# A new edge stage in a four-layer graph network: duplicate keys by products of sign codes, a scatter with split sources

## The chip, the cores and the metric

The kernel runs on one core of one Trainium2 chip. The metric is the time of one execution in microseconds (us). The engines are PE (TensorE, with PEld for its weight loads), DVE (VectorE), ACT (ScalarE), POOL (GpSimd) and SP, whose queue issues all transfers here. PE's clock has two levels, 1.2 and 2.4 GHz; the granted clock in a row is a share of the higher one.

## The reference

512 nodes with 512 features, and 16384 edges (src, dst, weight), sorted by dst. Four layers follow one another, each with a residual and a layer norm. The edges enter all of them, and the kernel turns them into two dense 512 x 512 matrices first: W_SD, the bias of the first attention, and A_SD, the number of edges between two nodes. The bias is *set*, not added: of several edges with the same (dst, src) the last one counts.

```python
src, dst = (edge_index[0], edge_index[1])
bias = jnp.full((n, n), NEG, dtype=x.dtype)
bias = bias.at[diag, diag].set(0.0)
bias = bias.at[dst, src].set(edge_weight.astype(x.dtype))
...
scores = jnp.einsum('hnd,hmd->hnm', q, k) / np.sqrt(HEAD_DIM)
attn = jax.nn.softmax(scores + bias[None, :, :], axis=-1)
```

The other layers are a mean over neighbours, a second attention with a mask, and a sum over neighbours; the change leaves them as they are.

## The kernel before

The program is written engine by engine, each with its own order, and semaphores between them. A ring of four PSUM banks carries all products of the dense layers in a fixed order (`ring_order`); `claim` takes the next bank when its last content is evacuated. Four other banks (`bank`) serve the edge stage and later the attention.

The 16384 edges are 128 tiles of 128. Two tiles make a group (64 groups); the edges are sorted by dst, so a group's dst lie in a window of 32 columns whose start is found at run time. Four groups make one round of the loops (16 rounds). The edge stage has these parts:

- **Keys** (L691 to L719). DVE casts src and dst to fp32, makes a key 512 dst + src, finds the range of each tile and from it the window starts, packed for the loops. SP stores the keys in DRAM (L324) and reads them back spread to all partitions, 8 MB in five pieces (L329). PE turns src, dst, weight and key so that an edge lies on a partition (L1023).
- **Duplicates** (L739 to L767). For every tile, DVE compares the key on the partition with the keys of this tile and the next one of its group, masked to later edges, and accumulates (L743, 128 instructions). An edge with a later equal key gets weight 0. Weights are kept as three bf16 parts, since a bf16 product would round them; POOL (L384) and DVE multiply them into one-hots of the window column (`rhs`).
- **Dense work beside it.** PE makes Q (L1031), K, V (L1002) and all 32 score products S (L1049); ACT evacuates them. The scores go to the tile G, in which the spread keys lie, so ACT waits for the compares.
- **Scatter** (L1052 to L1081, in loops). For each group PE multiplies a one-hot of the source (512 columns, in four blocks `b` of 128) with the window one-hots and the three weight parts, 24 bf16 matmuls. DVE makes one of the source one-hots (L781) and copies the window one-hots (L782); ACT makes the other in two steps (L552, L557). Then ACT copies the counts (L578), POOL adds them to A_SD (L438), and DVE clears the touched places of W_SD (L797) and adds the new weights (L804, the fold).

After the last fold `bias_built` lets PE turn W_SD and A_SD (L1008), DVE takes row minima of score plus bias (L847), ACT the exponentials, and the layers follow. SP loads x after `bias_built` too, POOL adds the bias to V (L429) in the middle of its weight products and makes the residual sums (L458) once x is there.

The order of PE's work around the change is the order of these lines: the range product, the turns of the edges, Q, the spread of the window starts, K, V, S, scatter. On SP's queue it is: edges, x and W_q by blocks, keys out, keys back with W_k and W_v between the pieces, W_o, W_1, vectors.

Of the kernel before, what the change touches and what calls it, by code (L numbers as in the profile page):

```python
# [7 lines left out]
I32 = mybir.dt.int32  # L8
# [17 lines left out]
KEY_CHUNKS = [0, 1, NI // 4, NI // 2, 3 * NI // 4, NI]  # L26
# [12 lines left out]

def ring_order():  # L40
# [9 lines left out]
    for b in range(NB):  # L50
        add("V", (b,), "A")
    for h in range(H):
        for b in range(NB):
            add("S", (h, b), "A")
# [66 lines left out]
def gnn_program(nc, a, out):  # L121

    ctx = ExitStack()
    with ctx:
# [6 lines left out]
        key_dram = nc.dram_tensor("key_scratch", [NT, P], FP32, kind="Internal").ap()  # L131
# [8 lines left out]
        WAF = sb("WAF", [P, 4 * NB * D + 2 * GI * 2 * WIN])  # L140

        WA = WAF[:, 0:4 * NB * D].rearrange("p (w b n) -> p w b n", w=4, b=NB)
        XT = WA[:, 3, :, :]

        rhs = WAF[:, :].bitcast(BF16).rearrange("p (t k n) -> p t k n", t=NT + 2 * GI, k=4)
# [47 lines left out]
        minus_src = sb("minus_src", [P, NT + 2 * GI])  # L193
        srcT, dstT, ewT, keyT = (tr[:, k, :] for k in range(4))
        later_mask = hf[:, 768:1024]
        later = hf[:, 1024:1152]
        w_rest = hf[:, 1152:1280]
        dstrel = hf[:, 1280:1280 + NT]
        parts = hf[:, 1408:1408 + 3 * NT // 2].bitcast(BF16).rearrange("p (t k) -> p t k", k=3)
        iota_w = hf[:, 1620:1636].bitcast(FP16)  # L200
        mm = hf[:, 1636:1638]
        base_bc = hf[:, 1638:1638 + NG]
        one = sb("one", [P, 1])
        rhs_now = sb("rhs_now", [P, GI, 2, 4, WIN], BF16)
        rf = RB[:, :, :].rearrange("p b n -> p (b n)")
        junk = rf[:, 0:1024].bitcast(BF16).rearrange("p (s e) -> p s e", s=2 * GI)
        distance = rf[:, 1024:1024 + (GI - 1) * N // 2].bitcast(FP16).rearrange("p (q n) -> p q n", q=GI - 1)
        oh = X[:, :, :].rearrange("p b n -> p (b n)").bitcast(BF16).rearrange("p (g t n) -> p g t n", g=4, t=2)
        iota_n = sb("iota_n", [P, N], FP16)
# [4 lines left out]
        bank = [ctx.enter_context(nc.psum_tensor(f"bank{i}", [P, 512], FP32)) for i in range(4)]  # L214
        ring_all = ctx.enter_context(nc.psum_tensor("ring", [P, R, 512], FP32))
        ring = [ring_all[:, i, :] for i in range(R)]
        group_bank = [bank[i][:, 0:NB * 2 * WIN].rearrange("p (b k n) -> p b k n", b=NB, k=2) for i in range(GI)]
# [11 lines left out]
        key_ready = sem("key_ready")  # L229
        key_stored = sem("key_stored")  # L230
        edges_float = sem("edges_float")
        tile_ranges = sem("tile_ranges")
# [7 lines left out]
        compared = sem("compared")  # L240
        flags_done = sem("flags_done")
        dst_relative = sem("dst_relative")
        src_turned = sem("src_turned")
        windows_ready = sem("windows_ready")
        rhs_pool = sem("rhs_pool")
        rhs_dve = sem("rhs_dve")
        renewed = sem("renewed")
        onehot_act = sem("onehot_act")
        distance_ready = sem("distance_ready")
# [44 lines left out]
        def blocks(w):  # L294
# [3 lines left out]
                     "col", "wqk2", "wv2", "wo2", "w12a", "w12b", "w22", "w3a", "w3b"] + VECTORS_0 + VECTORS_2 + \  # L298
                    [f"key{c}" for c in range(len(KEY_CHUNKS) - 1)]
# [7 lines left out]
        def _(sp):  # L307
# [15 lines left out]
            sp.wait_ge(key_ready, 1)  # L323
            sp.dma_start(key_dram, nat[:, 3, :]).then_inc(key_stored, 16)  # L324
            sp.wait_ge(key_stored, 16)
            flat = key_dram.rearrange("t e -> (t e)")
            for c in range(len(KEY_CHUNKS) - 1):
                part = slice(KEY_CHUNKS[c] * 2 * GI * P, KEY_CHUNKS[c + 1] * 2 * GI * P)
                load(f"key{c}", G[:, part], flat[part].partition_broadcast(P))  # L329
# [938 lines left out]
```

## Time and profile before

| | us |
|---|---|
| median of three runs | 592.97 |
| lowest and highest | 591.87, 593.33 |
| the profiled execution | 593.2 |
| its span in the trace | 591.3 |
| PE busy | 482.4 |
| DVE busy | 357.6 |
| ACT busy | 205.7 |
| POOL busy | 149.2 |

The span is the time from the first to the last instruction of the trace; the 1.9 us beside it lie around it. The busy times are sums over stages with different limits, so the share of an engine says little; the rows of single stages do. A matmul's duration in a row overlaps those of its neighbours, so a pitch, from one start to the next, is the better price. An fp32 matmul shows as two records (two passes). A row that ends in a bracket tells the idle time before it and what ended it.

### The profile page before, as it was taken

To read this page: it belongs to the slowest core of one execution; us is meant where nothing else is said; L and a number is where in the kernel's file an instruction comes from. 1 tells how busy PE (TensorE), PEld (TensorE's weight loads), DVE (VectorE), ACT (ScalarE), POOL (GpSimd) and SP (SyncE) were. 2 spreads that over 40 slices of the span, in tenths; PEclk is the share of its full clock that TensorE was granted. 3 is DMA by queue.
4 is the path that set the end of the run, shared out by engine and by line. 5 is a ranking of instruction groups with operands and counts; after the bars stand their busy time and mean duration, and the time that the engine had idled before them with its cause. 6 is when DMAs were issued, how large, how long until landed. Compare 5 with 4: busy or idle time off the path is not lost.

```text
span 591.3 us, 9566 instructions
## 1 busy us (share of the span) xinstructions
PE 482.4 (82%) x3050; PEld 286.8 (48%) x3050; DVE 357.6 (60%) x890; ACT 205.7 (35%) x408; POOL 149.2 (25%) x153
## 2 busy tenths in 40 slices
PE   4999465677675699999799899767768679999996
PEld 2444222677665599944344444445533234444442
DVE  6699998788887996457813410369992520064305
ACT  1244233998986757322210111313332111101110
POOL 6033330333332810012100610055554110011000
PEclk9999865756766869999899999989988859999998
DMA  6994000000000300439240020000000000000001
GB/s 190 395 414 174 0 1 0 3 0 0 0 0 24 119 1 2 172 114 355 71 125 1 0 72 0 0 0 1 1 0 1 0 0 1 1 0 1 0 1 71
DMA packets 14456, 34.14 MB, mean 58 GB/s; under 512 B 992, under 2 KB 1504, under 8 KB 13920
## 3 DMA queue, kind: packets, MB, share of 16 engines
q1 hardware_dynamic: 14432, 33.83, 15.8%
q8 instruction: 14, 0.23, 0.2%
q14 instruction: 10, 0.08, 0.0%
HBM read 32.71 MB, written 1.11 MB: 57 GB/s over the span
## 4 chain that ended last, share of the span: by engine, by line
PE 48%; DVE 26%; issue 11%; ACT 5%; DVEq 4%; DMA 3%; POOL 2%; ACTq 1%; POOLq 0%; SPq 0%
PE ring L1002 33%; PE bank L1105 5%; PE ring L1008 4%; DVE RB L743 4%; DVE G L951 3%; DVE G L947 3%; DVE G L962 3%; DVEq L743 2%; PE ring L1201 2%; DMA G<-key_scratch 2%; DVE st L889 2%; ACT RB L552 2%; PE ring L1188 1%; DVE G L847 1%; DVE W_SD L797 1%
## 5 line engine op out<-in xcount | busy, mean ns | idle before, releaser
L1063 PE MATMUL bank<-rhs_now,X 128*128 128x64 bf16 x512 | 58.3, 210 | 23.5 <-DVE rhs_now L782 22.3
L743 DVE SCALAR_TENSOR_TENSOR RB<-G,tr,HH 128x256 bf16<-128x256 f32 (+1 forms) x128 | 64.3, 566 | 9.0 <-DMA G<-key_scratch 5.1
L1063 PEld LDWEIGHTS bank<-rhs_now,X 128*128 128x128 bf16 x512 | 50.6, 102 | 29.7 <-DVE rhs_now L782 29.4
L1064 PE MATMUL bank<-rhs_now,X 128*128 128x32 bf16 x512 | 57.3, 204 | 0.0
L1065 PE MATMUL bank<-rhs_now,X 128*128 128x32 bf16 x512 | 56.3, 185 | 0.0
L458 POOL TENSOR_TENSOR RB<-X,vec 128x512 f32<-128x512 f32 x16 | 21.9, 1379 | 125.0 <-DVE X L898 117.6
L1065 PEld LDWEIGHTS bank<-rhs_now,X 128*128 128x128 bf16 x512 | 52.7, 121 | 0.0
L1064 PEld LDWEIGHTS bank<-rhs_now,X 128*128 128x128 bf16 x512 | 51.0, 103 | 0.0
L438 POOL TENSOR_TENSOR A_SD<-A_SD,HH 128x128 f32 x64 | 30.6, 478 | 74.6 <-ACT HH L578 63.9
L909 DVE TENSOR_TENSOR HH<-ring,RB 128x512 f32<-128x512 f32 x16 | 11.0, 686 | 61.3 <-PE ring L1002 46.3
L1049 PE MATMUL ring<-KB,QB 64*128 64x512 f32 x64 | 29.5, 747 | 20.2 <-ACT G L519 20.2
L533 ACT ACTIVATE sd<-mv,eps 128x1 f32<-128x1 f32 x32 | 9.4, 294 | 103.4 <-DVE mv L890 103.4
L1002 PE MATMUL ring<-WAF 128*128 128x512 f32 x96 | 42.1, 595 | 0.3 <-ACT WAF L519 0.2
L519 ACT ACTIVATE WAF<-ring 128x512 f32<-128x512 f32 x44 | 25.1, 589 | 49.5 <-PE ring L1008 49.5
L947 DVE TENSOR_REDUCE G<-ring 128x256 f32<-128x2048 f32 x8 | 18.3, 2292 | 36.8 <-PE ring L1188 36.7
L557 ACT ACTIVATE X<-RB,one 128x512 bf16<-128x512 f16 x51 | 36.8, 722 | 2.7
L552 ACT ACTIVATE RB<-iota_n,minus_src 128x512 f16<-128x512 f16 x51 | 36.2, 711 | 0.0
L491 POOL TENSOR_TENSOR G<-G 128x1024 f32<-128x1024 f32 x8 | 19.0, 2374 | 66.1 <-ACT G L642 46.2
L1105 PE MATMUL bank<-VB,WAF 128*128 128x64 f32 x256 | 32.7, 292 | 0.0
L1105 PEld LDWEIGHTS bank<-VB,WAF 128*128 128x128 f32 x256 | 32.6, 211 | 0.0
L1188 PE MATMUL ring<-QB,KB 64*128 64x256 f32 x128 | 18.5, 434 | 16.0 <-DVE G L951 15.1
L781 DVE TENSOR_SCALAR X<-iota_n,tr 128x512 bf16<-128x512 f16 x85 | 31.1, 382 | 0.1
(159 smaller groups left out, 965.2 us busy)
## 6 DMA issues: line engine op xcount, KB each, us to landing
G<-key_scratch SPq DMA_DIRECT2D x3, 2048.0 KB, 21.8
WAF<-in_wqkv SPq DMA_DIRECT2D x2, 1024.0 KB, 9.6
WB<-in_wo SPq DMA_DIRECT2D x2, 1024.0 KB, 17.0
WC<-in_w SPq DMA_DIRECT2D x2, 1024.0 KB, 17.0
WAF<-in_w SPq DMA_DIRECT2D x2, 1024.0 KB, 8.8
G<-in_w SPq DMA_DIRECT2D x1, 2048.0 KB, 14.7
G<-key_scratch SPq DMA_DIRECT2D x1, 1536.0 KB, 10.2
WAF<-in_xT SPq DMA_DIRECT2D x4, 256.0 KB, 5.4
```

The lines of the kernel that those rows point to most:

```text
L438: pool.tensor_tensor(win, win, cnt_g[:, q, :, :], ALU.add).then_inc(group_added, 1)
L552: act.activation(distance[:, q, :], iota_n[:, :], ACT.Abs, bias=minus_src[:, bass.ds(t, 1)]).then_inc(distance_ready, groups(q))
L557: act.activation(oh[:, q, 1, :], distance[:, q, :], ACT.Relu, bias=one[:, :], scale=-1.0).then_inc(onehot_act, groups(q))
L743: dve.scalar_tensor_tensor(out=junk[:, j, 0:width], in0=G[:, bass.ds((t0 + j) * P, width)], scalar=keyT[:, bass.ds(t0 + j, 1)], in1=later_ ...
L781: dve.tensor_scalar(oh[:, q, j, :], iota_n[:, :], srcT[:, bass.ds(t + j, 1)], None, ALU.is_equal)
L947: link(dve.tensor_reduce(top, ring_all[:, :, :].rearrange("p r (i n) -> p n (r i)", n=UN), AX.X, ALU.max))
L1002: last = nc.tensor.matmul(t[:, :], lhs(k), rhs_(k), start=(k == 0), stop=(k == n_k - 1))
L1049: nc.tensor.matmul(claim(("S", h, b))[:, :], QB[r, h // 2, b * P:(b + 1) * P], KB[r, h // 2, :], start=True, stop=True).then_inc(ring_full, 1)
L1063: nc.tensor.matmul(gb[:, b, :, :], src1, rhs_now[:, q, j, 0:2, :], start=(j == 0), stop=False)
L1064: nc.tensor.matmul(gb[:, b, 1, :], src1, rhs_now[:, q, j, 2, :], start=False, stop=False)
L1065: last = nc.tensor.matmul(gb[:, b, 1, :], src1, rhs_now[:, q, j, 3, :], start=False, stop=(j == 1))
L1105: last = nc.tensor.matmul(bank[b][:, g * HD:(g + 1) * HD], probsT[g % 2][:, m, b * P:(b + 1) * P], VB[:, m, g * HD:(g + 1) * HD], start=(m ...
```

## The change

The duplicate search moves from DVE to PE. Each key has 18 bits; as a vector of 18 signs (+16 or -16), two keys are equal exactly when their product is 18 x 256. Three more rows add the position of the edge, so that a product is positive only for an equal key that comes later. DVE makes the bits, SP stores the codes in DRAM as [tile, row, edge] and loads them back as 21 rows of all edges, once for each side of the product, each half of the tiles at another partition. PE puts two pairs of products behind every matmul of K, and DVE reduces each pair of two groups with one maximum over 768 columns.

The scatter splits a source into its low 7 bits (the 128 partitions of the result) and its high 2 bits, which join the window column: 4 x 32 = 128 columns. A group is then two bf16 matmuls for the counts and two fp32 matmuls for the weights, which are no longer in parts. The one-hots are made for eight tiles in one instruction, with two tiles innermost; ACT widens the source one-hots to fp32, and DVE multiplies the column one-hots by the weights. The loops are written out, and V and the scores S, which stood before the scatter, are spread over its 16 rounds. DVE clears from the counts in PSUM. POOL adds the bias of V after the counts, and W_o is loaded after the scatter, since its tile holds the widened one-hots.

The diff, cut to its core (the path for windows wider than 32 and the declarations are left out):

```diff
+def beside_scatter():
+    return [[("S", 2 * (c // NB), c % NB), ("S", 2 * (c // NB) + 1, c % NB)] + ([("V", c // NB)] if c % NB == 1 else [])
+            for c in range(NI)]
...
-            sp.wait_ge(key_ready, 1)
-            sp.dma_start(key_dram, nat[:, 3, :]).then_inc(key_stored, 16)
...
+            sp.wait_ge(code_ready, 3)
+            sp.dma_start(code_dram, code).then_inc(code_stored, 16)
+            load("wk0", WA[:, 1, :, :], blocks(a["wqkv0"][:, D:2 * D]))
+            sp.wait_ge(code_stored, 16)
+            for i in range(2):
+                of_half = code_dram[i * (NT // 2):(i + 1) * (NT // 2), :, :]
+                part = slice(i * 64, i * 64 + ROWS)
...
+                sp.dma_start(by_tile(rows_l[part, :]), of_half[:, 0:ROWS, :].rearrange("t k e -> k t e")
+                             ).then_inc(loads["rows"], 16)
+                sp.dma_start(by_tile(rows_r[i * 64 + 3:i * 64 + ROWS, :]),
+                             of_half[:, 3:ROWS, :].rearrange("t k e -> k t e")).then_inc(loads["rows"], 16)
+                sp.dma_start(by_tile(rows_r[i * 64:i * 64 + 3, :]),
+                             of_half[:, ROWS:ROWS + 3, :].rearrange("t k e -> k t e")).then_inc(loads["rows"], 16)
...
             sp.wait_ge(bias_built, 1)
             load("x", X[:, :, :], blocks(a["x"]))
+            load("wo0", WB[:, :, :], blocks(a["wo0"]))
...
             pool.engine_nop().then_inc(count_built, 1)
+            pool.wait_ge(loads["bv0"], 16)
+            for b in range(NB):
+                wait_emptied(pool, ("V", b))
+                pool.tensor_tensor(VB[:, b, :], VB[:, b, :], vec[:, slot["bv0"], :], ALU.add).then_inc(values_ready, 1)
...
+                for c in range(2):
+                    widen(c, c + 1, None)
+                for c in range(NI):
+                    take_beside(c)
+                    for q in range(GI):
+                        take_counts(c * GI + q, q)
+                    if c + 2 < NI:
+                        widen(c % 2, c + 3, (c + 1) * GI)
...
+            dve.tensor_scalar(hi_i, src_i, 7, 5, ALU.logical_shift_right, ALU.logical_shift_left).then_inc(edges_float, 1)
+            for k in range(CODE):
+                dve.tensor_scalar(bits_i[:, k, :], key_i, k, 1, ALU.logical_shift_right,
+                                  ALU.bitwise_and).then_inc(edges_float, 1)
...
+            dve.tensor_scalar(code[:, 3:ROWS, :], bits_i[:, :, :], 2.0 * BIT, -BIT, ALU.mult,
+                              ALU.add).then_inc(code_ready, 1)
...
-                        dve.scalar_tensor_tensor(
-                            out=junk[:, j, 0:width], in0=G[:, bass.ds((t0 + j) * P, width)],
-                            scalar=keyT[:, bass.ds(t0 + j, 1)], in1=later_mask[:, 0:width],
...
+            for p in range(PAIRS):
+                dve.wait_ge(pair_full, p + 1)
+                dve.tensor_reduce(later[:, 2 * p:2 * p + 2, :],
+                                  bank_all[:, p % 2 * 2:p % 2 * 2 + 2, 0:3 * P].rearrange("p r (c e) -> p r c e", e=P),
+                                  AX.X, ALU.max).then_inc(pair_taken, 1)
...
+            def hot(out_, keys):
+                return dve.tensor_tensor(out_, iota_2[:, :, :].rearrange("p (q n) j -> p q n j", q=1).broadcast_to(
+                    [P, GI, P, 2]), keys.rearrange("p (q n j) -> p q n j", n=1, j=2).broadcast_to([P, GI, P, 2]),
+                    ALU.is_equal)
...
+                for c in range(NI):
+                    word = dve.value_load(packed_i[0:1, c:c + 1], min_val=0, max_val=(1 << 28) - 1)
+                    g, more = c * GI, c + 2 < NI
+                    for q in range(GI):
+                        win = clear(g + q, q, window_start(word, q))
+                        if more and q == GI - 2:
+                            dve.wait_ge(group_full, g + GI)
+                            dve.wait_ge(src_wide_ready, c + 1)
+                            src_hots(c % 2, chunk(lo_key, c + 2))
+                        if more and q == GI - 1:
+                            weight_hots(c % 2, chunk(last_weight, c + 2), c + 3)
+                        fold(g + q, q, win)
+                        if more and q == GI - 2:
+                            dst_hots(c % 2, chunk(column_key, c + 2))
...
+            pe.wait_ge(loads["rows"], 96)
+            pe.wait_ge(src_turned, 1)
+            pe.wait_ge(dst_relative, 1)
+            def compare(p):
+                if p >= 2:
+                    pe.wait_ge(pair_taken, p - 1)
+                for i in range(2):
...
+                    nc.tensor.matmul(to[:, 0:2 * P], rows_l[part, e:e + P], rows_r[part, e:e + 2 * P], start=True,
+                                     stop=True)
+                    last = nc.tensor.matmul(to[:, 2 * P:3 * P], rows_l[part, e + P:e + 2 * P],
+                                            rows_r[part, e + P:e + 2 * P], start=True, stop=True)
+                last.then_inc(pair_full, 1)
...
+                for j in range(2):
+                    nc.tensor.matmul(counts, src_hot[:, slot_, q, :, j], dst_hot[:, slot_, q, :, j], start=(j == 0),
+                                     stop=(j == 1), skip_group_check=True)
+                for j in range(2):
+                    last = nc.tensor.matmul(weights, src_wide[:, slot_, q, :, j], weight_hot[:, slot_, q, :, j],
+                                            start=False, stop=(j == 1), skip_group_check=True)
...
+                for c in range(NI):
+                    beside(c)
+                    hots(c + 1)
                     for q in range(GI):
-                        group(g0 + q, g0 + q + 1, q)
+                        group(c * GI + q, q, c % 2)
```

## Rows read from the trace of the kernel before

**Rows 1.** The page's first line.
```profile
span 591.3 us, 9566 instructions
```
**Rows 2.** Busy times by stage: from:to, length, busy (count), PE clock, DMA share, GB/s.
```profile
16.50:103.00 86.50, 66.28 (x173) 29.23 (x172) 76.16 (x280) 29.26 (x50) 21.35 (x7) 0.83 0.41 162
103.00:189.40 86.40, 59.63 (x1518) 54.80 (x1514) 72.97 (x272) 75.94 (x160) 30.62 (x64) 0.64 0.00 1
```
**Rows 3.** Instructions grouped by line and shape: count, busy us, mean ns, idle before.
```profile
L947 DVE TENSOR_REDUCE G<-ring 128x256 f32<-128x2048 f32 x8 | 18.3, 2292 | 36.8 <-PE ring L1188 36.7
...
L372 DVE TENSOR_TENSOR WAF<-HH 128x1024 bf16<-128x1024 f16 x4 | 4.9, 1224 | 0.1
L781 DVE TENSOR_SCALAR X<-iota_n,tr 128x512 bf16<-128x512 f16 x85 | 31.1, 382 | 0.1
L438 POOL TENSOR_TENSOR A_SD<-A_SD,HH 128x128 f32 x64 | 30.6, 478 | 74.6 <-ACT HH L578 63.9 <-POOL A_SD L438 10.7
L642 ACT ACTIVATE G<-G 128x2048 f32<-128x2048 f32 x8 | 15.3, 1913 | 41.6 <-DVE G L951 41.6
```
**Rows 4.** The chain that ended last: start, length in us, what.
```profile
189.48 2.83 PE ring L1008 x12
...
216.12 3.58 PE bank L1105 x32
```
**Rows 5.** Instructions in order of time, the start: start, us, engine, line.
```profile
6.79 0.71 DVE L696 SCALAR_TENSOR_TENSOR HH<-HH 128x128 f32<-128x128 f32 x1
7.62 0.27 DVE L699 TENSOR_REDUCE HH<-HH 128x1 f32<-128x128 f32 x1
9.89 14.62 PE L1031 MATMUL ring<-WAF 128*128 128x512 f32 x32
14.00 0.23 DVE L724 TENSOR_SCALAR minus_src<-tr 128x136 f32<-128x136 f32 x1
```
**Rows 6.** Transfers: whole run, first 3 us, and single issues (KB, us to landing).
```profile
q1 hardware_dynamic: 14432, 33.83, 15.8%
q1 hardware_dynamic: 313, 0.15, 16.6%
X<-in_x SPq DMA_DIRECT2D x1, 1024.0 KB, 5.4
HH<-in_dst SPq DMA_DIRECT2D x1, 64.0 KB, 1.8
```
**Rows 7.** PE's instructions in order of time: K and V, and two of the scatter.
```profile
24.80 27.73 PE L1002 MATMUL ring<-WAF 128*128 128x512 f32 x64
...
150.41 0.19 PE L1063 MATMUL bank<-rhs_now,X 128*128 128x64 bf16 x1
...
150.49 0.19 PE L1063 MATMUL bank<-rhs_now,X 128*128 128x64 bf16 x1
```
**Rows 8.** PE alone in two stretches: length, busy (count), PE clock, DMA.
```profile
78.00:82.00 4.00, 4.00 (x9) 0.50 0.01 2
404.00:408.00 4.00, 2.29 (x22) 1.00 0.00 0
```
**Rows 9.** DVE in order of time, in the scatter and at its end.
```profile
116.30 0.29 DVE L797 SCALAR_TENSOR_TENSOR W_SD<-HH,W_SD 128x128 f32 x1 [0.75 <-issue]
...
117.46 0.28 DVE L797 SCALAR_TENSOR_TENSOR W_SD<-HH,W_SD 128x128 f32 x1
...
117.98 0.35 DVE L781 TENSOR_SCALAR X<-iota_n,tr 128x512 bf16<-128x512 f16 x1
...
188.46 0.29 DVE L804 TENSOR_TENSOR W_SD<-W_SD,bank 128x128 f32 x1
```
**Rows 10.** DVE and POOL in order of time, after the scatter: row minima, residual sums.
```profile
194.90 0.68 DVE L847 CUSTOM_DVE_ANT_0 G<-G,WAF 128x512 f32<-128x512 f32 x1
...
195.51 1.75 DVE L847 CUSTOM_DVE_ANT_0 G<-G,WAF 128x512 f32<-128x512 f32 x1
...
195.02 6.72 POOL L458 TENSOR_TENSOR RB<-X,vec 128x512 f32<-128x512 f32 x4 [7.36 <-DMA X<-in_x]
```

More of the change, by code:

```diff
@@ L25 @@
 NI = NG // GI
-KEY_CHUNKS = [0, 1, NI // 4, NI // 2, 3 * NI // 4, NI]
+CH = 2 * GI
+CODE = 18
+ROWS = CODE + 3
+BIT = 16.0
+PAIRS = NG // 2
 NEG = -1000000000.0
@@ L49, in ring_order @@
         add("KT", (b,), "A")
[L50 to L54, printed above, removed]
+    for names in beside_scatter():
+        for name in names:
+            add(name[0], name[1:], "A")
     for b in range(NB):
@@ L203, in gnn_program @@
[L203 to L209, printed above, removed]
+        loT, dstT, ewT, hiT = (tr[:, k, 0:NT] for k in range(4))
@@ L575, in take_counts, with widen, take_beside @@
-            def take_counts(g, t_next, q):
+            def widen(slot_, count, lap):
+                act.wait_ge(src_hot_ready, count)
+                if lap is not None:
+                    act.wait_ge(group_full, lap)
+                act.activation(src_wide[:, slot_, :, :, :], src_hot[:, slot_, :, :, :],
+                               ACT.Copy).then_inc(src_wide_ready, 1)
+            def take_beside(c):
+                for name in beside_scatter()[c]:
+                    if name[0] == "V":
+                        evac(name, VB[:, name[1], :])
+                    else:
+                        k = name[1] * NB + name[2]
+                        act.wait_ge(*((loads["rows"], 96) if k < H * NB // 2 else (pair_full, PAIRS)))
+                        evac(name, probs[:, k, :])
@@ L807, in _ @@
             wide = dve.value_load(wide_i[0:1, 0:1], min_val=0, max_val=1)
             with dve.If(wide < 1):
[L809 to L822 removed]
+                for c in range(2):
+                    src_hots(c, chunk(lo_key, c))
+                    dst_hots(c, chunk(column_key, c))
@@ new lines, in _ @@
+                for c in range(2):
+                    weight_hots(c, chunk(last_weight, c), c + 1)
+                for c in range(NI):
[12 more added lines that the diff above has]
+                            dst_hots(c % 2, chunk(column_key, c + 2))
@@ new lines, in _ @@
+            for b in range(NB):
+                t = claim(("KT", b))
+                for k in range(NB):
+                    last = nc.tensor.matmul(t[:, :], cols(WA[:, 1, :, :], k, b), XT[:, k, :], start=(k == 0),
+                                            stop=(k == NB - 1))
+                    if k == NB - 1:
+                        last.then_inc(ring_full, 1)
+                    for p in range(2):
+                        compare((b * NB + k) * 2 + p)
+            wait_emptied(pe, ("KT", NB - 1))
```

359 lines of the change are left out of this document (146 added, 213 removed).

## The prediction

> **What bounds the kernel now.** I read the busy times by stage first, then single stretches of each engine, and the chain of work that ended last for what comes after. The profiled execution has a span of 591.3 us [rows 1] and took 593.2 us in all; the median of the three runs is 592.97. Two long stages stand before the layers [rows 2]: the search for duplicate keys (16.5 to 103 us) and the scatter (103 to 189.4). In the search DVE is busy 76.2 of 86.5 us with its 128 compares: it is the bound, and PE and ACT do the scores in its shadow. In the scatter DVE is busy 73.0 and ACT 75.9 of 86.4 us, while PE runs its small products at a granted clock of 0.64. The last fold ends at 188.75 [rows 9], and in the chain PE's turns of the bias start at 189.48 [rows 4]; what follows the change hardly touches. So the time of the change is the time at which the last fold ends. Before, that is 188.75; I now rebuild it for the new kernel.
>
> **Codes.** The change puts 18 bit extractions and a conversion to bf16 ahead of everything. DVE's second cast still stands beside POOL's fills, so what follows it starts at 6.8 as L696 did [rows 5]. Then come one OR and two masks (0.25 each), 18 shifts, a few position rows and one conversion of 2304 elements. No row shows an integer shift on 128 elements; the nearest, the scale of 136 elements at L724, took 0.23 [rows 5], and I take 0.22, so 4.0 us for 18. The conversion lies between 1.3 us (0.23 scaled with half the rate of the reduce) and 2.6 us (1.12 ns an element, from the reduce of 2048 in 2.292, [rows 3]); I take 2.0. With some delay by POOL's selects (L696 took 0.71 beside them [rows 5]) the codes are ready at 14.5 (13 to 16.5). Two casts and the two reduces follow, 1.0 us, so the second reduce ends at 15.5 where it ended at 7.9, and the 32 Q passes that queue behind its product on PE (14.62 us from 9.89 [rows 5]) end at 32.1, not 24.5. The base product behind them, two DVE copies and PE's new wait on them make 33.1: this is the earliest start of the compares, hidden only if the codes land later.
>
> **Transfers.** The store is 786 KB; 1024 KB of x took 5.4 us [rows 6], so 4.3 and 0.3 of issue: stored at 19.1. W_k is queued behind it and ahead of the rows. The six loads have runs of 256 bytes: 2 x 64 x (21 + 18 + 3) = 5376 packets. In the first 3 us 313 packets took 16.6% of 16 engines [rows 6], 25.5 ns each (0.5 KB mean). If all 16 engines share alike, that is 336 packets, 8.6 us; but 21, 18 and 3 rows don't divide by 16, and if an engine takes whole rows the fullest has at least 2 + 2 + 1 rows of 64 packets in each half, 640, or 16.3 us. With equal shares of whole rows it is 3 + 2 + 1, 768 packets, 19.6 us. I take 18, and 1.8 us from issue to landing as for dst [rows 6]: 19.1 + 1.8 + 18 = 39 us. This is past 33.1, so it starts the compares. The upper bound is the mean packet of the whole run, 0.158 x 16 x 591.3 / 14432 = 104 ns [rows 6]: 80 us. The Trainium skill (DMA: Bandwidth & Descriptors, section "Why a DMA increments its semaphore by 16 and not by 1") says that a transfer runs on the largest number of engines up to 16 that divides the slowest dimension of both sides. By that the loads run on 7, 9 and 3 engines, and the sum would be 1.6 us longer; no row here has such a transfer to show it.
>
> **Compares.** Sixteen steps each hold one K product and two pairs. An fp32 product of 512 columns takes two passes, 27.73 us for 64 [rows 7], so 0.87. A pair has 768 columns of bf16; three matmuls with 128 columns went in 0.08 us [rows 7], so 0.48 (0.32 if the three weight loads in that row are what cost). PE: 0.87 + 0.96 = 1.83 a step. DVE reduces 768 elements a pair from PSUM: between the 128 of L699 in 0.27 [rows 5] and the 2048 of L947 in 2.292 [rows 3] that is 0.94, 0.90 start to start, 1.80 a step. Only two pairs fit the banks and a K product stands between them, so the two don't overlap wholly: 2.1 a step (1.85 to 2.3), 33.6 us. PE idles from 33 to 39 first. In the trace it was granted 0.50 (1.2 GHz) at 78 to 82 us, just after a long wait for DVE, though it was busy 4.00 of 4.00 us [rows 8]; I add 3.0 us for two steps at the low level, and 0.9 for the last reduce. The compares end at 39 + 37.5 = 76.5.
>
> **Scatter, start.** DVE: 0.8 us of small flag operations, four one-hots and one weight product. A one-hot has 1024 16-bit elements. The nearest rows are L372, 1024 elements in 1.224 with a 32-bit key, and L781, 512 elements 16-bit to 16-bit in 0.382 [rows 3] and 0.35 at its quickest [rows 9]; here all operands are 16-bit too, so I take twice 0.35, 0.7. The weight product has fp32 operands: 1.22. Less overlaps, 4.6 us: first group at 81.1. The Trainium skill (VectorE: DVE Perf Modes, section "The perf-mode tier table") gives a two-input operation twice the rate where all is bf16 in SBUF; L372, with its 32-bit key, shows the plain rate only, and by that rate each one-hot would cost 0.5 us more.
>
> **Scatter, a chunk of four groups.** DVE: a clear and a fold start 0.52 us apart from the next operation (117.46 to 117.98 [rows 9]), four times 2.08; two one-hots and a weight product 2.62; a register load of the window word, of which the 0.75 of issue ahead of 116.30 [rows 9] is an upper bound, 0.3; and waits beside POOL: a two-input operation of DVE took 0.68 alone and 1.75 beside POOL's adds [rows 10], and POOL adds counts four times a chunk, so at most 4 x 0.478 [rows 3]; most will miss each other, I take 0.4. Together 5.4 (4.7 to 6.4). PE: two scores 1.73, and per group two bf16 products 0.16 and two fp32 products of 128 columns. For those, 32 passes of 64 columns took 3.58 us [rows 4], 0.11 each and no dearer at 128 (a quarter of 0.433), so 0.44. A chunk is 1.73 + 4 x 0.60 = 4.1, under DVE's 5.4. ACT: two evictions of 512 elements, a widening of 1024 and four copies of 128, at 1.913 for 2048 [rows 3] and some 0.1 more for each small one, 3.1: hidden, though its order (widen, evict, copy counts) makes it nearly late. Four chunks carry a V product, 3.47 more, between two groups on PE's queue. From the last fold of a chunk PE needs 0.60 + 1.73 + 3.47 + 0.60, ACT's copy 0.25 and some 0.3 of signals, 6.95, before DVE can clear: 1.55 of stall each. The last two chunks make no one-hots and go at PE's 4.1. Sum: 14 x 5.4 + 2 x 4.1 + 4 x 1.55 = 90.0, and the last fold ends at 171.1, or 17.7 us earlier than before.
>
> **What goes elsewhere.** S and V were free before, under DVE's compares; now they are on PE beside the scatter, which is why PE comes near DVE. The four bias adds of V on POOL, of the shape of the residual adds (6.72 us beside DVE [rows 10]), move behind the counts; PE needs them before it turns the probabilities, behind 32 turns of bias and counts, so they about fit, but DVE's row minima start beside them, at 1.75 instead of 0.68 [rows 10], and POOL's residual adds come later: +1.5 us (0 to 4). W_o is loaded after the scatter now, behind x on SP's queue, and used only after the whole attention: 0. The other loads of SP's queue (W_v, vectors) stand behind the rows; V is the first to need one, in the second chunk: 0.
>
> **Rivals.** *PE's clock.* PE's work in compares and scatter is 16 x 1.83 + 16 x 4.1 + 4 x 3.47 = 109 us at 2.4 GHz against 126.6 us that I give these stages. If the clock stays as low as in the scatter before, 0.64 [rows 2], PE is the bound: 170 us, so 620 us. It turns slower than before from a mean of 0.76. For it: PE idles before each stage. Against it: at 404 to 408 it was granted 1.00 with 2.29 of 4.00 us busy [rows 8], and a PE that is behind is busy all the time. *Slow rows.* If the fullest engine's 768 packets cost over 44 ns, the compares start so late that all is lost; half way between that and the 104 ns bound it is 616 us. *All goes well.* Even spread (compares from 33.1), no low clock, no port waits, cheap pairs: 560 us. *The one-hots don't gain from 16 bits.* At L372's 1.22 instead of 0.7 that is 1.0 us more a chunk, less stall at V, 2 us at the start: 589 us; the change would do only half of what it says.
>
> **How the numbers follow.** 593.2 - 17.7 + 1.5 = 577.0; the median lies 0.2 lower, which I leave out. Chances: forecast 0.43 (568 to 586 of its own), all goes well 0.20, plain-rate one-hots 0.12, clock 0.12, slow rows 0.13. The range from 555 to 608 leaves out the heavier halves of the last two and a little below. A change under 0.3% (1.8 us) can't be told from none. Faster: 0.43 + 0.20 + 0.11 = 0.74; same 0.05; slower 0.21.
>
> **What would show it.** The load of the rows should land near 39 us and the compares run to 76, two reduces every 2.1 us; two-input one-hots should take 0.7 us; DVE should have the fewest waits in the scatter except after V; the last fold should end near 171. A landing past 55, or PE without idle time at a clock under 0.8 in the scatter, would make the prediction wrong upwards; a landing at 30 or chunks of 4.7 downwards.

## The result, and the profile after

The changed kernel takes 595.6 us (median; 593.2 to 599.4), the kernel before 593.3 in the same comparison: ratio 1.0044, 95% interval 1.0025 to 1.0063. It is slower by 0.4%, where I had forecast it faster by 2.7%. The profiled execution of the changed kernel took 599.4 us, the longest of its runs, so its rows show 3.8 us more than the median.

The page's first line, which answers to [rows 1]:

```profile
span 597.3 us, 6327 instructions
```

Instructions grouped by line, from 37 to 95 us: the compare stage, which takes the place of DVE's compares (count, then busy us, mean ns, and the idle time ahead with what ended it):

```profile
L1056 PE MATMUL ring<-WA 128*128 128x512 f32 x32 | 33.1, 1139 | 4.7 <-DMA G<-code_scratch 4.7
L750 DVE TENSOR_REDUCE HH<-banks 128x6 f32<-128x768 f32 x32 | 29.2, 953 | 30.1 <-PE banks L1049 30.1
L1047 PE MATMUL banks<-G 21*128 21x256 bf16 x64 | 21.6, 409 | 0.0
```

PE waits 4.7 us for the rows of codes and then, by these rows, never again. DVE's reduce costs 0.95 us as forecast, but DVE is idle for as long as it works, always for PE. So PE is the bound here. Why it is so slow stands in the busy times by stretch (length, busy and count of PE, PEld, DVE, ACT, POOL, granted clock, DMA share, GB/s); the second row is the scatter:

```profile
42.00:90.00 48.00, 48.00 (x142) 19.36 (x140) 25.91 (x29) 2.06 (x3) 0.00 (x0) 0.50 0.13 46
99.00:194.70 95.70, 80.53 (x476) 52.77 (x476) 67.78 (x171) 46.31 (x113) 33.36 (x65) 0.95 0.01 2
```

PE is busy 48.00 of 48.00 us and is granted 0.50, 1.2 GHz, all that time. One step of the stage, in order of time (start, us, engine, line):

```profile
41.03 2.08 PE L1056 MATMUL ring<-WA 128*128 128x512 f32 x2
43.04 0.39 PE L1047 MATMUL banks<-G 21*128 21x256 bf16 x1
...
44.43 2.08 PE L1056 MATMUL ring<-WA 128*128 128x512 f32 x2
```

A K product takes 2.0 us instead of 0.87, the compares of a step 1.4, and a step 3.4 us from K product to K product. The scatter's own start and end, on DVE:

```profile
95.13 2.50 DVE L729 TENSOR_TENSOR X<-iota,HH 128x1024 bf16<-128x1024 bf16 x4 [1.10 <-issue]
97.55 2.35 DVE L741 TENSOR_TENSOR RB<-X,HH 128x1024 f32<-128x1024 bf16 x2
...
194.45 0.29 DVE L783 TENSOR_TENSOR W_SD<-W_SD,banks 128x128 f32 x1
```

The last fold ends at 194.74, where it was 188.75 [rows 9]. From there to the end of the span it is 402.6 us in both traces (597.3 - 194.74 and 591.3 - 188.75): the whole loss of these two executions (6.0 us; 2.3 by the medians) stands ahead of the last fold.

### The profile page after: what moved, and what is told of

Read it like the earlier page. It is cut to its first block, busy times and chain, and to the rows that moved or that the text cites. A ratio compares the mean times of both kernels' runs of the same rounds, so it can differ in the third digit from the quotient of the medians.

```text
span 597.3 us, 6327 instructions
## 1 busy us (share of the span) xinstructions
PE 504.1 (84%) x2026; PEld 282.8 (47%) x2026; DVE 317.3 (53%) x571; ACT 155.4 (26%) x322; POOL 134.4 (22%) x150
## 4 chain that ended last, share of the span: by engine, by line
PE 62%; DVE 24%; issue 4%; ACT 2%; DMA 2%; SPq 2%; DVEq 1%; POOL 1%; POOLq 0%
PE ring L997 35%; PE ring L1056 5%; PE banks L1133 5%; PE ring L1003 4%; DVE G L946 3%; DVE G L942 3%; PE banks L1091 3%; PE banks L1047 3%; DVE G L957 2%; PE ring L1229 2%; PE ring L1216 2%; DVE X L729 2%; DVE st L884 2%; DVE W_SD L783 2%; DVE G L842 2%
## 5 line engine op out<-in xcount | busy, mean ns | idle before, releaser
L448 POOL TENSOR_TENSOR RB<-X,vec 128x512 f32<-128x512 f32 x16 | 21.7, 1360 | 118.9 <-DVE X L893 117.5
L750 DVE TENSOR_REDUCE HH<-banks 128x6 f32<-128x768 f32 x32 | 29.2, 953 | 30.1 <-PE banks L1049 30.1
L1091 PE MATMUL banks<-RB,WB 128*128 128x128 f32 x256 | 44.1, 300 | 0.0
L1056 PE MATMUL ring<-WA 128*128 128x512 f32 x32 | 33.1, 1139 | 4.7 <-DMA G<-code_scratch 4.7
L1091 PEld LDWEIGHTS banks<-RB,WB 128*128 128x128 f32 x256 | 36.3, 202 | 0.0
L1133 PE MATMUL banks<-VB,WA 128*128 128x64 f32 x256 | 32.6, 292 | 0.0
L1133 PEld LDWEIGHTS banks<-VB,WA 128*128 128x128 f32 x256 | 32.4, 210 | 0.0
L1216 PE MATMUL ring<-QB,KB 64*128 64x256 f32 x128 | 19.1, 443 | 14.7 <-DVE G L946 13.7
L997 PE MATMUL ring<-WA 128*128 128x512 f32 x64 | 31.0, 632 | 0.3 <-ACT WA L509 0.2
L997 PE MATMUL ring<-WC,WA 128*128 128x512 f32 x64 | 28.7, 595 | 2.0 <-ACT WA L509 2.0
L997 PE MATMUL ring<-G,WA 128*128 128x512 f32 x64 | 29.2, 610 | 0.8 <-DVE HH L904 0.8
L997 PE MATMUL ring<-G 128*128 128x512 f32 x64 | 27.7, 594 | 0.8 <-ACT G L511 0.8
L842 DVE CUSTOM_DVE_ANT_0 G<-G,WA 128x512 f32<-128x512 f32 x32 | 27.9, 912 | 0.1
```

Of the source, the lines that this page charges most:

```text
L448: pool.tensor_tensor(out_, x_, vec[:, slot[vector], :], ALU.add).then_inc(resid_ready, 1)
L750: dve.tensor_reduce(later[:, 2 * p:2 * p + 2, :], bank_all[:, p % 2 * 2:p % 2 * 2 + 2, 0:3 * P].rearrange("p r (c e) -> p r c e", e=P), AX ...
L842: dve.tensor_tensor_reduce(out=probs[:, k, :], in0=probs[:, k, :], in1=B_DS[:, b, :], scale=-1.0, scalar=3.0e38, op0=ALU.add, op1=ALU.min, ...
L997: last = nc.tensor.matmul(t[:, :], lhs(k), rhs_(k), start=(k == 0), stop=(k == n_k - 1))
L1056: last = nc.tensor.matmul(t[:, :], cols(WA[:, 1, :, :], k, b), XT[:, k, :], start=(k == 0), stop=(k == NB - 1))
L1091: last = nc.tensor.matmul(weights, src_wide[:, slot_, q, :, j], weight_hot[:, slot_, q, :, j], start=False, stop=(j == 1), skip_group_chec ...
```

## The experiments

Two theories stood against each other at first. **A, height:** compares that use 21 of PE's 128 rows keep the clock at its lower level, however busy PE is. **B, history:** the stage only keeps the level that the gap ahead of it (4.7 us without work) left behind. A third, **C**, was that the exchange of banks between PE and DVE sets the pace. Ratios are against the kernel before, whose medians were 593 to 594 us each time; the profile of each run has its own time base.

**K products first.** The K loop moves ahead of the wait for the rows; the compares run alone.

```diff
+for b in range(NB): product(("KT", b), ...)
 pe.wait_ge(loads["rows"], 96)
-for b ...: for k ...: matmul(K); compare(..); compare(..)
+for p in range(PAIRS): compare(p)
```

> All 16 K products run at once behind the Q products, before the rows are awaited; the 32 pairs of compares run alone behind them. Theory A (the compares, 21 of 128 rows high, keep TensorE at 1.2 GHz though it is busy all the time, and the K products between them pay for it): K runs at the level Q leaves behind (2.4 GHz), 33 to 49 us; the compares alone still show a granted clock of 0.50, but 0.64 us of TensorE work for a pair is less than VectorE's 0.95 us reduce, so they end at about 49 + 32 x 0.95 = 79.5 us instead of 93.2, and the run is 13 to 15 us shorter than the changed kernel: 581 to 584 us. Theory C (the handing over of banks between TensorE and VectorE, not the clock, sets the pace): 1.7 us for a pair stays, the compares end at 49 + 55 = 104 us, and the run is some 10 us longer.

Measured: 577.7 us, ratio 0.9715 (0.9679 to 0.9752). Two stretches, in the columns of above:

```profile
42.00:46.00 4.00, 4.00 (x11) 1.56 (x10) 0.00 (x0) 0.69 (x2) 0.00 (x0) 1.00 1.05 386
58.00:62.00 4.00, 3.52 (x19) 1.51 (x17) 4.00 (x5) 0.00 (x0) 0.00 (x0) 0.50 0.00 0
```

The K products ran at 1.00; once the compares were alone the clock fell to 0.50, but DVE is busy 4.00 of 4.00 us and sets the pace, 0.93 us a pair, so the level costs nothing there. The stage ended at 76.2, 3 us before the 79.5 that A gave, since the compares began at 45.9 and not at 49. C falls: the banks change hands fast enough. That the compares alone lose the level suits A, and B too if PE's short pauses beside DVE count as a gap.

**Compares of 64 rows.** Rows 21 to 63 of each half are zeroed by ACT, and the compares read 64 rows.

```diff
-part = slice(t // (NT // 2) * 64, t // (NT // 2) * 64 + ROWS)
+part = slice(t // (NT // 2) * 64, t // (NT // 2) * 64 + 64)
```

> The compares read 64 rows instead of 21 (rows 21 to 63 of each half are zeros, written early by ScalarE), so the same products are counted with three times the rows of the array in use; order and count of instructions stay. Theory A (height): the granted clock in the compare stage rises above 0.50; at 2.4 GHz a step takes about 2.0 us (VectorE's two reduces) instead of 3.4, the stage ends near 72 us and the run is up to 20 us shorter (577); with 64 of 128 rows still half empty, a part of that. Theory B (the level is left over from the idle 4.7 us before the stage): no change, 0.50 throughout, 595 to 599 us.

Measured: 595.1 us, 1.0010 (0.9985 to 1.0035); the clock at 42 to 90 us:

```profile
42.00:90.00 48.00, 48.00 (x143) 19.77 (x142) 26.07 (x29) 2.06 (x3) 0.00 (x0) 0.50 0.14 52
```

Nothing changed. Three times the height was not enough, which spoke for B.

**The gap filled.** Six products whose result is overwritten run between the last Q product and the wait for the rows; nothing else changes.

```diff
+t = claim(("KT", 0))
+for k in range(6): matmul(t, WA[:, 0, ...], XT[:, k % NB, :], start=True, stop=True)
 pe.wait_ge(loads["wk0"], 16)
 pe.wait_ge(loads["rows"], 96)
```

> Six further 128x512 fp32 products, whose result is overwritten, fill the 4.7 us in which TensorE waits for the rows; the interleaving of K products and compares stays. Theory B (the stage only inherits a low level from the idle gap): the stage starts at 2.4 GHz and stays there, a step takes 2.0 us, the compares end near 71 us, and the run takes about 577 us. Theory A (height): the stage starts at 2.4 GHz and falls back to 0.50 within some microseconds; the run is 0 to 4 us shorter than the changed kernel, 593 to 599 us.

Measured: 573.9 us, 0.9657 (0.9614 to 0.9700). The fill on PE and the first K product behind it, in order of time:

```profile
31.75 5.42 PE L1035 MATMUL ring<-WA 128*128 128x512 f32 x12
38.03 1.10 PE L1059 MATMUL ring<-WA 128*128 128x512 f32 x2 [0.86 <-issue]
```

and the stage, in the columns of above:

```profile
42.00:66.00 24.00, 23.39 (x123) 10.05 (x122) 22.35 (x26) 2.06 (x3) 0.00 (x0) 1.00 0.30 100
```

The same instructions of the stage, in the same order, with a gap of 0.86 instead of 4.7 us ahead of them, run at 1.00 to the end. So 5.4 us of work that is thrown away save 21.7 us (573.9 against 595.6). A in the form that I had given it falls: 21 rows don't drag the level down as long as PE has next to no pause. B is right that the level depends on what lies ahead of the stage.

**The fill behind the wait.** The same six products, but after the rows have landed.

```diff
 pe.wait_ge(loads["rows"], 96)
 ...
+t = claim(("KT", 0))
+for k in range(6): matmul(t, WA[:, 0, ...], XT[:, k % NB, :], start=True, stop=True)
```

> The same six overwritten products as in the run that filled the gap, moved behind the wait for the rows: the gap of 4.7 us is back, and the stage begins with an unbroken run of 128-row products. If the interleaved stage only keeps the level that it finds (it held 1.00 in the run with the gap filled, and 0.50 in the changed kernel), and an unbroken run of 128-row products brings the level back (as the first V product of the scatter does, some 5 us after its start), then the six take about 10 us, the stage behind them runs at 1.00 and takes 33 us: its end is near 81 us and the run takes about 583 us. If the gap by itself decides, the stage stays at 0.50: 37.7 + 12 + 55.5 = 105 us, and about 607 us.

Measured: 580.5 us, 0.9797 (0.9764 to 0.9830). PE waits 6.0 us here, starts at the lower level, and gets the higher one back while the six products run:

```profile
38.00:42.00 4.00, 3.78 (x5) 1.75 (x6) 0.00 (x0) 0.00 (x0) 0.00 (x0) 0.50 1.02 368
42.00:46.00 4.00, 4.00 (x9) 1.77 (x9) 0.00 (x0) 0.00 (x0) 0.00 (x0) 0.88 1.06 385
46.00:50.00 4.00, 3.83 (x21) 1.66 (x20) 2.63 (x4) 0.00 (x0) 0.00 (x0) 1.00 0.46 164
```

So the gap is not fatal by itself: an unbroken run of 128-row products brings the level back, and the narrow mix then keeps it. What the mix of the changed kernel didn't do in its 55 us is bring it back.

**Six K products in the gap, no extra work.**

```diff
+for n in steps[:6]: step(*n)              # K products 0 to 5
 pe.wait_ge(loads["rows"], 96)
+for i, n in enumerate(steps[6:]): step(*n); 3 or 4 pairs of compares
```

> No extra work: the first six K products run in the gap, the other ten stand between the 32 pairs of compares. TensorE has 10 x 1.0 + 32 x 0.34 = 21 us of work at 2.4 GHz in the 31 us that VectorE's reduces take. If the level holds with TensorE busy 70 per cent of the stage, the stage is VectorE's, ends near 70 us, and the run takes about 572 us. If the pauses let the level fall, TensorE needs up to 42 us from 38 us on, the stage ends near 80 us, and the run takes about 582 us, as where all K products went ahead.

Measured: 587.1 us, 0.9895 (0.9851 to 0.9938), later than either expectation. The stage enters at 1.00 and loses it:

```profile
38.00:42.00 4.00, 3.21 (x22) 1.63 (x22) 2.72 (x4) 0.46 (x1) 0.00 (x0) 1.00 0.98 317
42.00:46.00 4.00, 3.28 (x12) 1.11 (x10) 2.75 (x3) 0.23 (x1) 0.00 (x0) 0.57 1.05 385
46.00:50.00 4.00, 3.58 (x14) 1.57 (x12) 2.78 (x3) 0.00 (x0) 0.00 (x0) 0.50 0.50 167
```

With fewer K products between the compares, PE pauses for DVE (3.21 of 4.00 us busy), the next stretch is at 0.57, and from there on it is 0.50. PE (3.5 of 4.00) and DVE (2.8 of 4.00) both wait for each other then, and the stage ends at 83.5.

**Compares of all 128 rows.** As with 64 rows, but each compare reads both halves at once; gap and order are those of the changed kernel. The same kernel ran twice.

```diff
-part = slice(t // (NT // 2) * 64, t // (NT // 2) * 64 + ROWS)
+part = slice(0, P)
```

> What is left of the theory of height: the compares use all 128 rows (both halves of the row tensors at once, so each product is the sum of two tiles' products and the compare no longer says which edge is a duplicate: that part of the computation is not the reference's). Gap, order, counts and columns are those of the changed kernel. If height keeps the level at 1.2 GHz, the granted clock now rises above 0.50 in the stage, steps fall from 3.4 to about 2.0 us and the run takes about 578 us. If height has no part in it, 0.50 and 3.4 us a step stay: 593 to 599 us.

> The run with compares over all 128 rows and the gap left in, timed: if its one profile shows what the kernel does, 570 to 576 us, 4 per cent under the changed kernel; if the level came back by chance in that one execution, about 595 us.

Measured: 572.8 us in the first, a single execution; 574.5 us in the second, 0.9687 (0.9643 to 0.9732), 3.5 to 5 us less than the first of the two expectations gave. In the first, after a wait of 5.2 us:

```profile
38.00:42.00 4.00, 4.00 (x12) 2.02 (x13) 1.31 (x2) 0.00 (x0) 0.00 (x0) 0.50 0.88 302
42.00:46.00 4.00, 3.87 (x21) 2.09 (x20) 2.80 (x4) 0.00 (x0) 0.00 (x0) 0.75 1.05 402
46.00:66.00 20.00, 19.12 (x112) 9.97 (x111) 19.65 (x23) 2.06 (x3) 0.00 (x0) 1.00 0.18 68
```

The level is down at first, as in the changed kernel, but now it comes back in the middle of the mix and stays. Between this run and the one with 64 rows the height differs, and how many of the rows hold data. One of the two, or something that goes with it, counts after all for the way up.

And for the way down: the six K products in the gap, with compares of 128 rows.

> As the run with six K products ahead (where the level fell at some 42 us with TensorE busy about 70 per cent of the stage), but with compares over all 128 rows (sums of two tiles' products; the compare no longer says which edge is a duplicate, so that part is not the reference's). If height counts for keeping the level as it did for raising it, the stage stays at 1.00, is paced by VectorE's reduces, ends near 70 us, and the run takes 570 to 575 us. If the pauses alone decide, the level falls as before: end near 83 us, 585 to 588 us.

Measured: 570.6 us, 0.9629 (0.9588 to 0.9670). The stage, which at 21 rows fell to 0.50:

```profile
42.00:70.00 28.00, 20.66 (x130) 10.58 (x128) 26.33 (x32) 1.44 (x3) 0.00 (x0) 1.00 0.21 76
```

PE is busy less (20.66 of 28.00), and keeps 1.00. The pauses that these rows show didn't decide alone.

**Rows addressed, or rows with data?** In the first variant, all 128 rows are read but only 21 hold data; in the second the left rows of each half lie in a place of their own with zeros around them, and the right rows fill both halves. The edit of the second:

```diff
-rows_l = G[:, 8192:12288].bitcast(BF16)
+rows_l = [G[:, 4096 * (i + 1):4096 * (i + 2)].bitcast(BF16) for i in range(2)]
-matmul(to, rows_l[part, e:e + P], rows_r[part, ...])       # 21 rows
+matmul(to, rows_l[half][0:P, e:e + P], rows_r[0:P, ...])   # 128 rows, zeros around
```

> The compares address all 128 rows, but only the 21 rows of the first half hold data, all others are zero (the second half's rows go to an unused place, and its tiles read the first half's, so their flags are not the reference's). If the rows addressed count, the level comes back some 6 us into the stage as in the runs with 128 rows, a step takes 2.0 us, and the run takes 571 to 577 us. If the rows that hold data count, the stage stays at 0.50 and 3.4 us a step: 592 to 599 us.

> The whole computation, gap left in, with compares over 128 rows: the left rows of the two halves lie in two places, zeros around them, so that the other half's right rows meet zeros. If the rows addressed count: 571 to 577 us. If the rows with data on both sides count (21): 592 to 599 us.

Measured: 572.1 us for the first, a single execution; 573.1 us for the second, 0.9693 (0.9630 to 0.9757). The first, in two stretches:

```profile
38.00:42.00 4.00, 3.79 (x12) 1.93 (x12) 0.99 (x2) 0.00 (x0) 0.00 (x0) 0.58 0.96 299
42.00:46.00 4.00, 3.83 (x22) 2.01 (x22) 3.93 (x5) 0.00 (x0) 0.00 (x0) 1.00 1.05 399
```

The second reads 0.50, 0.79 and 1.00 in the stretches that begin at 38, 42 and 46 us. In this mix the rows that the compares address decide, zeros or not.

That the height itself is the cause does not follow, for two reasons. The first is in the trace of the kernel before, where a run of score products of 64 rows, with none of 128 among them, begins at the lower level; below it is PE in two stretches (columns as in [rows 8]):

```profile
76.15 8.90 PE L1049 MATMUL ring<-KB,QB 64*128 64x512 f32 x16 [10.25 <-ACT G L519]
```

```profile
81.00:82.00 1.00, 1.00 (x4) 0.50 0.00 0
83.00:84.00 1.00, 1.00 (x4) 0.99 0.00 0
```

Products of 64 rows (fp32 with 512 columns, so not the compares' form) did bring the level back there, some 7 us after their start. The second reason is a difference in the weight loads. Those ahead of the first compare and of the second K product, in the changed kernel and then in the first run with 128 rows, both granted 0.50:

```profile
39.64 0.10 PEld L1047 LDWEIGHTS banks<-G 21*128 21x128 bf16 x1 [1.50 <-issue]
41.03 0.50 PEld L1056 LDWEIGHTS ring<-WA 128*128 128x128 f32 x2 [0.30 <-issue]
```

```profile
38.88 0.15 PEld L1053 LDWEIGHTS banks<-G 128*128 128x128 bf16 x1 [0.52 <-issue]
40.91 0.55 PEld L1062 LDWEIGHTS ring<-WA 128*128 128x128 f32 x2
```

In the changed kernel both loads start together with their own products (39.65 and 41.03). With 128 rows they start 0.85 and 0.10 us ahead of them (39.73 and 41.01), and the first step takes 3.11 us instead of 3.32. The run with 64 rows is like the changed kernel here (load and compare both at 40.79). So where products of unlike height alternate, PE waits for weights twice a step, and its busy time of 48.00 us covers these waits. Whether the level hangs on the height or on the waits that come with it, no run separates; compares as tall as the K products remove both.

**Left rows of 24.** The left side's loads carry three rows more that no product reads.

```diff
-sp.dma_start(by_tile(rows_l[part, :]), of_half[:, 0:ROWS, :] ...)
+sp.dma_start(by_tile(rows_l[i * 64:i * 64 + ROWS + 3, :]), of_half[:, 0:ROWS + 3, :] ...)
```

> The left side's row loads carry 24 rows instead of 21 (three that no product reads). If the packets of a transfer are dealt out to the largest number of engines up to 16 that divides its rows, 24 rows go to 12 engines with 128 packets each where 21 go to 7 with 192: the fullest engine of all six loads has about 640 packets instead of 768, and at 25 ns each the rows land about 3 us earlier, at 34.5 us instead of 37.6; the compares then start and end 3 us earlier and the run takes about 594 us. If the packets are spread evenly, 7% more of them land no earlier: 597 to 599 us.

Measured: 593.8 us, 1.0005 (0.9974 to 1.0037): by time it can't be told from the changed kernel, whose interval overlaps (1.0025 to 1.0063). The trace tells more. The issue of a right-side load on SP's queue, in order of time, in the changed kernel:

```profile
18.66 3.16 SPq L353 DMA_DIRECT2D G<-code_scratch  x1
```

and its busy times from 18 to 30 us:

```profile
18.00:30.00 12.00, 12.00 (x26) 5.13 (x26) 2.60 (x13) 0.00 (x0) 0.00 (x0) 1.00 0.72 150
```

The same two views of this run:

```profile
18.70 2.08 SPq L352 DMA_DIRECT2D G<-code_scratch  x1
```

```profile
18.00:30.00 12.00, 12.00 (x26) 5.12 (x26) 2.61 (x13) 0.14 (x1) 0.00 (x0) 1.00 0.90 187
```

SP issues faster, as it would if the queue drained faster: the 16 engines are busy 0.90 instead of 0.72 of the time, and the six loads are issued from 18.27 to 30.27 instead of 18.25 to 32.72: 12.0 us for 14.5, the ratio of 640 to 768 packets, although there are more packets in all (and W_k shares the queue at first). It is no accident of one execution: the three later runs with 24 left rows read 0.88 to 0.91 in the same stretch, all runs with 21 read 0.69 to 0.73. The first K product starts at 36.2 instead of 37.7, half of the 3 us that I had expected. An even spread is ruled out; so is a share of whole rows over all 16 engines, by which 21 rows would cost what 24 do.

**Putting it together.** Left rows of 24, four K products in the gap, and two V blocks beside the compares, so that PE has no pause there; then a third V block in the pause of 5.2 us ahead of the scatter's first group; then tall compares on top.

```diff
+for n in steps[:4]: step(*n)              # K products 0 to 3
 pe.wait_ge(loads["rows"], 96)
+for i, n in enumerate(steps[4:]): step(*n); 1 or 2 pairs of compares   # 12 K, 8 V
-beside_scatter: V block c // 4 in chunks 1, 5, 9, 13
+beside_scatter: V block 2 in chunk 9, 3 in chunk 13           # second kernel: in 0 and 8
```

> Left rows of 24; four K products in the gap that is left, the other twelve and two of the four V blocks (eight products) between the pairs of compares: 20 x 1.0 + 10.9 = 31 us of TensorE work at 2.4 GHz beside VectorE's 31 us. If the level holds, the stage runs from 36 to about 68 us, and the scatter loses two of its four V stalls (1 to 2.6 us each): 566 to 571 us. If the level falls, the stage needs 62 us and the run takes about 598 us.

> As the run with 24 left rows, four K products ahead and two V blocks in the compare stage, but the third V block runs ahead of the first group, in the 5.2 us in which TensorE waits for the first one-hots, and not in a later chunk. Its 3.7 us fit into the gap; the scatter loses one V stall (0.9 us), and its first chunk is no longer entered at 1.2 GHz (0.50 from 74 to 82 us there), worth 1 to 3 us: 568 to 571 us. If the level falls all the same in the 1.5 us that stay empty, only the stall goes: 571 us.

> The same tall compares in the run with four K products in the gap, two V blocks beside the compares and one ahead of the first group. There the level held in the stage already at 21 rows, so tall compares should give nothing: 567 to 571 us. If they help at the stage's end too, where that run showed 0.69 at 70 to 74 us, about 1 us less.

Measured: 572.1 us, 0.9641 (0.9623 to 0.9659), just above its range; 569.4 us, 0.9605 (0.9566 to 0.9644), as expected; 564.6 us, 0.9530 (0.9498 to 0.9562), below its range. In the last one the stage and the start of the scatter never leave 1.00, where the second showed 0.69 at 70 to 74:

```profile
70.00:74.00 4.00, 2.53 (x6) 0.76 (x4) 3.75 (x6) 2.88 (x4) 0.00 (x0) 1.00 0.00 0
74.00:78.00 4.00, 3.70 (x28) 2.80 (x28) 2.55 (x7) 1.81 (x6) 1.37 (x3) 1.00 0.01 4
```

The flags behind the compares start 4.0 us earlier there (68.64 against 72.64, their second operation), which is most of the difference; I had not expected tall compares to help a stage that was at 1.00 already. The waits for weights can account for it: in the second run PE is busy 31.70 of 32.00 us from 38 to 70, and from a K product to its first compare it is 1.06 us, from the last compare to the next product 0.15; with tall compares it is 0.91 and 0.06. By estimate that is 0.24 us in each of twenty steps, 4.8 us. This version is 4.7% faster than the kernel before, and 5.1% faster than the changed one (0.9530 / 1.0044).

## Why the prediction was wrong, step by step

The ends of the stages, in us of each profiled execution:

| step | forecast | changed kernel | gap filled |
|---|---|---|---|
| rows landed, first K product | 39 | 37.7 | 38.0 |
| compares end | 76.5 | 93.2 | 70.6 |
| first group of the scatter | 81.1 | 99.0 | 76.4 |
| last fold ends | 171.1 | 194.7 | 168.7 |
| from there to the end of the span | 404.1 | 402.6 | 403.4 |

**The step that failed is one term of the compares: "3.0 us for two steps at the low level".** All sixteen steps ran at it: 55.5 us instead of 37.5, 18.0 of the 23.6 by which the last fold is late (the rest: 1.3 earlier by the landing, 1.2 and 5.7 later by preparation and scatter). I had the row in hand, PE granted 0.50 while busy 4.00 of 4.00 us after a wait [rows 8], and read it as a short delay. The rival *PE's clock* was held down to 0.12 with "a PE that is behind is busy all the time"; the 48.00 busy us at 0.50 show that this argument is empty. The Trainium skill (TensorE: Matmul & The Clock Gate, section "Part 1: The HAM clock gate (the "warmup" mystery)") has the throttled level as the default, released by sustained matmul activity; the runs agree for unbroken products of 128 rows and differ for the narrow mix, which by PE's busy time was sustained and was not released. What in the mix withholds the level stays open, as said above; that it does so after a gap of 4.7 us and not after 0.86 us is shown. The rival's threshold was met by luck: I had it turn slower than before at a mean of 0.76, and from 37.7 to 194.7 us the mean is 0.77, for +6.0 us of span. But it had PE as the bound of both stages at one low level; PE was at 0.50 in the compares, where it was the bound, and at 0.95 in the scatter, busy 80.53 of 95.70 us. Its chance was too small, because I had tied it to the whole of both stages; the compares alone were enough.

**Transfers: right in time, in part by luck.** The codes were stored at 18.2 (19.1 forecast; the store took 4.1 us for 4.3), the rows landed at 37.6 (39). From store to landing that is 19.4 us, and the sum had 19.8, with 18 us taken between the prices of 640 and of 768 packets. The fullest engine's 768 packets are borne out by the run with 24 rows; at my 25.5 ns each they would have made 21.4 us, so a packet was cheaper than I had it. The Trainium skill (DMA: Bandwidth & Descriptors, section "Why a DMA increments its semaphore by 16 and not by 1") gives the largest divisor up to 16; this case's trace now agrees, by 12.0 for 14.5 us.

**Codes and Q: right.** Eighteen shifts took 2.94 us (4.0 forecast), the conversion 1.35 (2.0); the casts beside POOL took longer. The Q products end at 32.6 (32.1). One reading of the kernel before was loose: its 128 compares are 64.3 of DVE's 76.2 busy us; nothing in the sum hangs on it.

**Scatter: 5.8 us of preparation for 4.6, and 95.7 us for 90.0.** In the preparation I had left out the 1.10 us of issue ahead of the first one-hot. DVE's terms hold: a one-hot 0.72 (0.7), a weight product 1.21 (1.22), a plain chunk 5.52 (5.4). So the rival of one-hots at the plain rate is out. What was off most is the V block: 1.55 us of stall forecast for each, 6.2 for four, where the chunks with one are 2.3, 2.6, 0.9 and 2.6 us longer than plain ones, 8.4 in all; 0.12 us in each of 14 plain chunks make 1.7 more. The starts of the weight products, chunk after chunk, across a V block in the changed kernel:

```profile
124.08 1.21 DVE L741 TENSOR_TENSOR RB<-X,HH 128x1024 f32<-128x1024 bf16 x1
129.59 1.21 DVE L741 TENSOR_TENSOR RB<-X,HH 128x1024 f32<-128x1024 bf16 x1
137.70 1.21 DVE L741 TENSOR_TENSOR RB<-X,HH 128x1024 f32<-128x1024 bf16 x1
```

The last two are 8.11 apart, the first two 5.51, and PE was granted 0.62 and 0.52 at 126 to 130 us. With the gap filled the same place reads 106.86 to 113.31, 6.45. So a V block costs 0.9 us at 2.4 GHz and 2.6 where the level dips first; the forecast lay between. Why it dips in one execution and not in another is not settled: with left rows of 24 the same code of the scatter took 91.2 us from first clear to last fold, where the profiled execution of the changed kernel took 93.8.

**The tail: 1.5 us forecast, which can't be told.** The bias adds of V do stand behind the counts now, at 193.82 for 4.95 us, and the residual adds at 200.17. The tail is 402.6 us before and after, but over the traces of the other runs, whose tails have the same code as the changed kernel's, it goes from 399.7 to 403.4.

With the gap filled, the clock in the compares is close to what I had taken it to be (two steps low; here none), and the median of 573.9 is 3 us short of my 577. Some of that agreement is two misses that cancel: its compares and preparation took 38.4 us where I had 42.1, its scatter 92.3 where I had 90.0. Still, no other part was off by enough to turn the sign; the sign hung on the level at which PE came out of a pause of 4.7 us.

## What to carry to other kernels

A stretch in which TensorE is busy all the time at half the clock need not recover: here the compares stayed at 0.50 for 55 us, while other stretches that were as busy came back within some 7 us. Look at what stands ahead of it, and at whether narrow products alternate with tall ones in it. Work of 128 rows in the pause ahead (21.7 us gained by products whose result is thrown away), or rows of zeros that make the narrow products as tall as the others (22.5 us, 573.1 against 595.6), gave back more here than the whole change had lost; zeros up to 64 rows gave nothing. And a filled gap is not all: with six K products ahead, the stage behind them paused and lost the level, and only 8.5 of the 21.7 us were gained.

## What the hardware showed that I had not expected

- Two lasting states of one instruction sequence: the same K products and compares of 21 rows ran at 1.00 for 32 us behind a gap of 0.86 us, and at 0.50 for 55 us behind a gap of 4.7 us, busy 48.00 of 48.00.
- In a mix with products of 128 rows, the height of the others bears on the clock: with compares of 21 or 64 rows the level didn't come back, with 128 it did, zeros included, and it was kept at 20.66 busy of 28.00 us, where at 21 rows it fell after a stretch with 3.21 of 4.00. Products of 64 rows by themselves did bring it back (the kernel before, at 83 us), so the height alone is not shown to be the cause.
- A compare takes the same time with 21 and 64 rows (0.409 and 0.411 us for 256 columns at 0.50). A change of height costs time: beside K products of 128 rows the weights of a compare of 21 or 64 rows are not loaded ahead, and a step is 0.2 us longer than with 128 rows at either level.
- Three rows more made a transfer of 21 rows quicker (issue of all six loads 12.0 instead of 14.5 us).
